# Every position of a four-layer transformer kernel's step table set anew

## The reference

```
def layer0(x, t):
    h = ada_rms(x, t, ln1_w, ln1_tw)
    q, k, v = rope(h @ Wq.T), rope(h @ Wk.T), h @ Wv.T      # 8 heads of 64, one key head
    x = x + softmax(q @ k.T / 8) @ v @ Wo.T
    h = ada_rms(x, t, ln2_w, ln2_tw)
    return x + silu(h @ Wg.T) * (h @ Wu.T) @ Wd.T           # 2048 hidden
def layer1(x, t):
    gamma1, gamma2, scale1, scale2, shift1, shift2 = silu(t) @ Wada.T + bada
    q, k, v = (ln(x) * (1 + scale1) + shift1) @ Wqkv.T + bias   # 16 heads of 32, q and k normalised
    x = x + (softmax(q @ k.T + attn_bias) @ v @ Wproj.T + bproj) * gamma1
    return x + (gelu_tanh((ln(x) * (1 + scale2) + shift2) @ Wfc1.T + bfc1) @ Wfc2.T + bfc2) * gamma2
def layer2(x, t):
    h = ln(x) * (1 + scale) + shift
    q, c = rope(h @ Wq.T), h @ Wkd.T
    k, v = rope(c @ Wku.T), c @ Wvu.T                        # 4 key heads
    return x + softmax(where(mask, -inf, q @ k.T / sqrt(32))) @ v @ Wo.T
def layer3(x, t):
    y = concat_e(gelu(x_e @ W1_e + b1_e) @ W2_e + b2_e)       # 8 experts of 64 features
    return x + silu((ln(y) * ln_g + ln_b) * (1 + scale) + shift) @ out_W + out_b
```

## Time and profile before

| what | value |
| --- | --- |
| median of 3 runs | 1981.3 us (1979.28 to 1987.42) |
| the profiled execution's own time | 1980.78 us |
| its span | 1979.0 us |
| PE busy | 1866.0 us, 94% |
| DVE busy | 1142.5 us, 58% |
| ACT busy | 1029.2 us, 52% |
| POOL busy | 817.1 us, 41% |
| mean granted TensorE clock | 0.972 |

### The profile page before, as it was taken

The page is one execution under the profiler, slowest core; times in us unless marked ns, Lnnn a source line. Parts: engine busy times, 40 slices in busy tenths (PEclk is TensorE's granted clock), DMA queues, the critical chain, the costliest instruction groups (busy, mean ns, idle before and its releaser), DMA issues.

```text
span 1979.0 us, 35216 instructions
## 1 busy us (share of the span) xinstructions
PE 1866.0 (94%) x12840; PEld 1492.0 (75%) x12840; DVE 1142.5 (58%) x3224; ACT 1029.2 (52%) x2478; POOL 817.1 (41%) x1094
## 2 busy tenths in 40 slices
PE   5789999999999999999899999999999989979877
PEld 3568878888888888888678888878886778856465
DVE  4767554643553356544774577576565785466453
ACT  3544433433343344543555466466477566467865
POOL 4466772211213344233678464237343432243320
PEclk9889999999999999999999999999999989989988
DMA  7335787556445544436454534442534534322321
GB/s 246 110 128 176 268 292 251 189 196 214 162 148 192 181 161 139 158 135 234 145 171 165 203 134 150 139 151 85 195 119 150 173 106 163 136 80 91 107 65 54
DMA packets 98651, 314.76 MB, mean 159 GB/s; under 512 B 11568, under 2 KB 13232, under 8 KB 96944
## 3 DMA queue, kind: packets, MB, share of 16 engines
q1 hardware_dynamic: 98480, 312.52, 45.8%
HBM read 242.48 MB, written 66.58 MB: 156 GB/s over the span
## 4 chain that ended last, share of the span: by engine, by line
PE 78%; DVE 9%; POOL 4%; ACT 4%; issue 3%; DMA 2%; SPq 0%; POOLq 0%; DVEq 0%; ACTq 0%
PE B L360 72%; PE B L363 6%; POOL SS L375 1%; DVE FB L381 1%; DVE T L378 1%; ACT SS L366 1%; POOL R L378 1%; DVE SS L384 1%; POOL W L378 1%; ACT GF L366 1%; DMA ST<-in_wpack 1%; ACT FB L366 1%; DVE HA L381 1%; ACT L366 1%; DVE Y L378 1%
## 5 line engine op out<-in xcount | busy, mean ns | idle before, releaser
L375 POOL TENSOR_SCALAR SS<-SS,NM 128x256 f32<-128x256 f32 (+1 forms) x640 | 299.2, 484 | 703.1 <-DVE NM L390 702.8
L360 PE MATMUL B<-HM,W 128*128 128x512 f32 x2304 | 533.2, 391 | 3.8 <-DVE X L381 1.8
L360 PEld LDWEIGHTS B<-HM,W 128*128 128x128 f32 x2304 | 431.7, 188 | 96.2 <-issue 4.1
L360 PE MATMUL B<-G,W 128*128 128x512 f32 x1536 | 382.4, 398 | 1.5 <-POOL W L378 0.4
L360 PEld LDWEIGHTS B<-G,W 128*128 128x128 f32 x1536 | 280.5, 188 | 61.3 <-issue 2.6
L366 ACT ACTIVATE SS<-SS,NM 128x256 f32<-128x256 f32 (+1 forms) x512 | 240.4, 471 | 106.2 <-DVE NM L384 105.7
L360 PE MATMUL B<-HA,W 128*128 128x512 f32 x864 | 229.7, 417 | 11.9 <-DVE HA L378 3.0
L360 PEld LDWEIGHTS B<-HA,W 128*128 128x128 f32 x864 | 166.3, 199 | 56.1 <-issue 14.6
L363 PE MATMUL B<-ident,SS 128*128 128x128 f32 x1152 | 170.1, 285 | 16.1 <-POOL SS L375 15.3
L378 DVE TENSOR_TENSOR G<-FB,G 128x512 fp32r<-128x512 f32 x128 | 101.3, 795 | 130.0 <-ACT G L366 130.0
L363 PEld LDWEIGHTS B<-ident,SS 128*128 128x128 f32 x1152 | 133.4, 145 | 53.2 <-issue 31.6
(11 more groups left out here) (111 smaller groups left out, 2674.8 us busy)
## 6 DMA issues: line engine op xcount, KB each, us to landing
W<-kept SPq DMA_DIRECT2D x357, 512.0 KB, 4.3
kept<-W SPq DMA_DIRECT2D x119, 512.0 KB, 4.8
ST<-in_wpack SPq DMA_DIRECT2D x139, 256.0 KB, 2.9
Y<-in_adaw SPq DMA_DIRECT2D x12, 1024.0 KB, 5.9
FB<-FB SPq DMA_DIRECT2D x52, 64.0 KB, 3.3
X<-in_xT SPq DMA_DIRECT2D x1, 3072.0 KB, 13.8
out_xT<-X SPq DMA_DIRECT2D x12, 256.0 KB, 2.2
FB<-in_pos SPq DMA_DIRECT2D x4, 256.0 KB, 5.2
```

The lines of the kernel that those rows point to most:

```text
L360: return self.real.matmul(*a, **k) if self.real is not None else self
L375: return self.real.tensor_scalar(*a, **k) if self.real is not None else self
```

## The change

Only the numbers in `PLACE` differ; there are 3,724 of them before and after, and no line outside the table changes. Two of its lines show the form:

```diff
 PLACE = {
-    "once": [2, 0, 40, 125, 843, 909, 1214, 2226, 5, 89, 322, 400, 436, 511, 572, 614, 678, 734, 809, 848],
+    "once": [1, 10, 39, 230, 845, 943, 1214, 2226, 9, 91, 323, 400, 436, 513, 572, 614, 678, 735, 804, 848],
...
-    "k": [30, 31, 34, 35, 39, 46, 172, 173, 182, 183, 199, 212, 420, 421, 427, 441, 471, 481, 748, 749, 755, 762, 779,
+    "k": [31, 33, 35, 37, 40, 46, 170, 174, 182, 183, 199, 204, 420, 421, 427, 441, 471, 479, 749, 750, 756, 763, 778,
```

More of the change, by code:

```diff
@@ L30 @@
 PLACE = {
-    "once": [2, 0, 40, 125, 843, 909, 1214, 2226, 5, 89, 322, 400, 436, 511, 572, 614, 678, 734, 809, 848],
-    "ada": [12, 13, 14, 15, 121, 122, 131, 132, 395, 396, 407, 408, 433, 434, 473, 475, 496, 497, 503, 504, 545, 546,
[31 rows of a table removed]
-    "scores": [43, 50, 68, 86, 108, 134, 161, 192, 204, 220, 250, 279, 328, 353, 409, 435, 484, 508, 561, 593, 651,
[5 rows of a table removed]
-    "softmax": [44, 45, 47, 54, 55, 51, 52, 53, 62, 63, 56, 57, 61, 72, 74, 64, 65, 71, 82, 83, 73, 75, 80, 90, 92, 84,
[55 rows of a table removed]
-    "values": [69, 70, 76, 87, 91, 93, 109, 110, 111, 135, 143, 156, 162, 165, 166, 184, 185, 188, 203, 206, 207, 219,
[15 rows of a table removed]
@@ new lines @@
+    "ada": [13, 14, 15, 16, 123, 147, 177, 181, 395, 396, 407, 408, 433, 434, 473, 475, 484, 486, 494, 495, 545, 546,
[31 rows of a table added]
+    "scores": [44, 54, 70, 88, 108, 141, 158, 191, 203, 219, 249, 279, 318, 355, 410, 435, 485, 511, 567, 601, 653,
[5 rows of a table added]
+    "softmax": [45, 48, 50, 55, 56, 47, 49, 53, 64, 65, 57, 58, 62, 72, 79, 66, 67, 73, 86, 87, 74, 75, 82, 95, 99, 76,
[55 rows of a table added]
+    "values": [68, 71, 78, 97, 98, 103, 112, 113, 129, 144, 156, 160, 157, 164, 171, 178, 179, 189, 202, 206, 207, 218,
[15 rows of a table added]
+    "stats": [3, 4, 5, 6, 7, 8, 83, 84, 90, 115, 116, 118, 290, 292, 306, 316, 326, 328, 617, 618, 626, 627, 658, 660,
[12 rows of a table added]
@@ L235 @@
-    "last": [2875, 2876, 2888, 2889, 2898, 2899, 2903, 2904, 3432, 3425, 3433, 3434, 3442, 3443, 3461, 3467, 3552,
-        3553, 3564, 3565, 3572, 3573, 3580, 3581, 3697, 3699, 3702, 3704, 3711, 3713, 3714, 3715, 3716, 3717, 3718,
[9 rows of a table added]
+    "down": [320, 321, 335, 337, 345, 346, 362, 363, 405, 406, 418, 419, 428, 429, 446, 448, 474, 480, 481, 487, 498,
[13 rows of a table added]
+    "first": [2707, 2708, 2709, 2711, 2725, 2727, 2726, 2729, 2736, 2741, 2744, 2746, 2753, 2754, 2759, 2760, 3282,
[4 rows of a table added]
+    "second": [2722, 2728, 2732, 2734, 2735, 2743, 2756, 2757, 2758, 2766, 2770, 2775, 3293, 3295, 3297, 3298, 3305,
+        3306, 3321, 3324, 3326, 3329, 3330, 3339, 3453, 3457, 3459, 3465, 3466, 3467, 3473, 3480, 3495, 3491, 3494,
+        3497, 3606, 3607, 3608, 3613, 3615, 3620, 3621, 3622, 3630, 3626, 3628, 3631, 3635, 3637, 3640, 3651, 3653,
+        3663, 3659, 3660, 3667, 3670, 3671, 3672],
```

17 lines of the change are left out of this document (6 added, 11 removed), and 366 rows, old and new, of the table PLACE.

## The result

The changed kernel takes 1912.8 us (median of 4 runs, 1911.06 to 1913.76) against 1982.1 for the kernel before in the same series: ratio 0.9646, 95% interval 0.9624 to 0.9668. The forecast was 1963 us, with a range of 1942 to 1985. The sign was right; the gain is 69 us where 17.3 had been worked out.

The account below looks back on a forecast made before the run. PE, busy 1866.0 of 1979.0 us, was taken to set the time. Terms -2.0 - 1 - 5 - 6 - 2.5 - 3.5 - 1.3 + 4 = -17.3 from 1980.8 gave 1963 us, own range 1952 to 1971, with rivals 1942 to 1985.

Parts of the forecast that it names:

- The start: Program start, to the first nfin: fewer transfers ahead of X and earlier additions bring nfin from 19.77 to 17.7; -2.0 us.
- 48 to 160 us: Early patch with 17.3 us of PE idle time to share out: -1 us, ends -6 and +7.
- First MLP of layer 1: 940 to 970 us: the PT copy and last nfin and nlo move ahead on DVE, shortening PE's waits; -5 us.
- Between layers 1 and 2: Normalisation at 1575 to 1594 us: products moved into PE's waits ahead of nvar and nbc, less slow clock; -6 us.
- 1725 to 1772: Layer 2's last part: values, nvar and nbc moved around PE's waits, a fifth of the clock loss regained; -2.5 us.
- 1860 to 1900: Last normalisation but one: nbc ahead of a values and a turn, exp no longer behind a copy; -3.5 us.
- the end: Program end: the first last no longer stands behind the 1.28 us wait for the other half's nbc; -1.3 us.
- All other stretches are shuffled too, and there PE can only lose: Outside the named patches: a sum of short new PE waits, +4 us by estimate, ends 0 and +20.
- The splits: GpSimd's weight splits delaying DVE instructions on SBUF alone: stays in DVE's idle time, 0 us, ends 0 and -15.
- Rival 3: Whole kernel: the gain is twice as large because the slow clock goes with the waits; 1943 us, chance 0.18.
- Rival 1: At each patch: waits move to the next step instead of going; about 1979 us, no change, chance 0.17.
- Rival 2: scores pairs of layers 1 and 2: products hold banks longer and wait for a max; 2000 us, slower, chance 0.13.

Follow-up runs that it names:

- The start alone: The kernel before with the new order only in steps 0-43 (to about 33 us): ratio 1.0006, no change.
- one_move: The kernel before with one step moved: reciprocal and scaling of group 121 six steps earlier, ahead of the third quarter of nfin; ratio 0.9992.
- moves3: The kernel before with three steps moved: reciprocal and scaling of group 121, and two sums of the next normalisation, put ahead of nfin quarters; ratio 1.0000.

## Why the prediction was wrong

**The start (-2.0; none).** Its steps came as written: first PE row 9.38 (9.9 forecast), first `nfin` 17.40 (17.7). What failed is the silent step after them, that 2 us won at 18 us are still won later. The start alone measured 1.0006. PE waits 4.06 us for the first remainder and 3.77 us for the keys, and at the first `scores` 0.4 to 0.5 us of it are left.

**48 to 160 us (-1; -15 by the traces, -10 measured alone).** The row of 17.3 us of idle time was read, and then a third of it at the far end was all that was allowed, weighed against three `scores` that moved the wrong way. The lower bound of -6 was an argument about how much may go, not read from any row. PE's waits from 40 to 160 us are of ten kinds, none of more than 4.1 us in all, so no single row named the gain.

**First MLP of layer 1 (-5; -7.3).** Right in its mechanism: copy and `nlo` ahead on VectorE, the wait 0.44 us, the clock 1.00. With only the other engines' queues new PE's wait for the copy is 0.40 us, with only PE's order new 2.95: that wait is VectorE's order, as the term assumed. But the first of these kernels loses 4.4 us right ahead of the stretch and wins 6.3 in it, so from 935 to 1000 us it gains only 1.9; the full gain needs both here too.

**Between layers 1 and 2 (-6; -5.0).** Right: 0.9 us was forecast ahead of `nvar`, 0.61 is there; 0.8 ahead of `nbc`, none is there, and the `scores` before it wait 0.62.

**1725 to 1772, 1860 to 1900 and the end (-2.5, -3.5, -1.3; -6.6, -8.5, -1.0).** The moves named were right, the sizes too small by more than half in the first two. At the first `last` the 6.96 us went altogether; the prediction had counted two moved steps on PE (2.4) and 1.1 on ScalarE, each by itself. It also named `nhi` as the end of the chain. In the kernel before the first high and low part were ready at 1897.3 us; PE went on at 1899.63, 0.1 us behind the fourth FB<-Y,B, the last reader of the bank that `nbc` had written:

```profile
1896.60 0.69 DVE L378 TENSOR_TENSOR ZL<-FB,ZH 128x512 fp32r<-128x512 f32 x1 [3.50 <-ACT ZH L366]
...
1898.85 0.68 DVE L378 TENSOR_TENSOR FB<-Y,B 128x512 f32<-128x512 f32 x1
```

The end came out near its number by luck: the 1.28 us went as written, but `nvar` waits 0.99 longer.

**"All other stretches are shuffled too, and there PE can only lose" (+4; -26 to -28).** This step failed most. It said that PE idled 57 us outside the patches, "mostly at start and end". 35 of them do lie there (0 to 48 and 1900 to 1979 us); but 13.0 lay in 970 to 1575 us and 8.2 in 1772 to 1860, and one window over each would have shown it, as one over 160 to 940 us did. The first of them, at clock 1.00 and 98% busy, looks closed at a glance. Its waits, seventeen of 0.2 to 2.3 us in 565 us, are just what a new order of the whole list can take away, and it took all but 0.6 us. The term was put at a loss without a reason that a row gave; the kernel with the new order everywhere but in the named stretches measured -28.

**The splits (0; perhaps 7).** The Trainium skill's rule ("SBUF — State Buffer", "Who interferes with whom") that such work on VectorE and GpSimd excludes each other is borne out by the 30.8 us of VectorE's busy time. That it "stays in its idle time" is not: shorter splits give the kernel before 13 us, 3.8 of them at the one place that the prediction named and the rest elsewhere, though a part may be weights that come sooner.

**The rivals.** Rival 3 came nearest with 1943 us, and by luck. Its sum, -42, was for the start, the four later patches and the end; the traces give 0.9 - 7.3 - 5.0 - 6.6 - 8.5 - 1.0 = -27.5 for those stretches, and the rest of the gain lies where it had counted -1 or +4. Its mechanism, that slow products leave with the waits, is there in the mean clock (0.972 to 0.987); that they are worth their time by themselves is not what the transposes show. Rival 1 is real for a step moved alone (one_move, moves3) and false for the whole list. Rival 2, the banks, did not come as a loss of the new order: PE's waits for a `max` are 1.3 us. PE's order alone was slower by 41 us, half of its added idle time through inputs; the part of the banks in the rest is open.

## What to carry to other kernels

A wait in front of a saturated engine can be the nearest of several chains that end close together. Here moving the one step that the trace named moved the wait by one row, and only the neighbourhood reordered on all queues gave the time back. So judge such a change by all idle time of the stretch, not by the wait that one explains, and call a stretch closed only when its window says so; even that is no upper bound, since 993 to 1558 us gained 17.7 us with 12.7 idle. Orders of two engines are one object: half of a good order was 2% slower than the old one here, so undo such a change by place in the list, not by engine.

## What the runs showed of the hardware

- Transposes of the identity that fill PE's waits keep the granted clock at its higher level (mean 0.972 to 0.986, `nvar` 1.87 to 1.05 us), and the time did not fall by more than the measurement can tell (1.0018 in the kernel before; 0.9634 against 0.9646 in the changed one).
- Making 119 GpSimd instructions half as long (1.29 to 0.62 us) took 31 us off VectorE's busy time without a change to VectorE's program; one VectorE group beside such an instruction took 1.22 us instead of 1.88.
- The kernel before spreads over 8 us between runs (1979.3 to 1987.4) and the changed one over 3 (1911.1 to 1913.8). In traces of kernels that share the old order at 33 to 163, 947 to 993 and 993 to 1558 us these places take up to 3 us more or less from run to run, though nothing differs there; a difference of 2 us at one of them says nothing by itself.
